# Rings of four blocks, looped edge stages, and own rows added on VectorE in a four-layer graph network

## The chip, the cores and the metric

The kernel runs on one core of a Trainium2 chip. The core has five engines that work side by side, each with its own stream of instructions: PE (TensorE, the matrix engine), DVE (VectorE), ACT (ScalarE), POOL (GpSimd) and SP (SyncE, which here only issues DMAs). Sixteen DMA engines move data between DRAM and the on-chip memories (SBUF, and PSUM for PE's results). Engines wait for each other and for DMAs by semaphores. The metric is the device time of one launch in microseconds (us); lower is better.

## The reference, cut to what matters

There are 100,000 nodes with rows of 128 float32 values, and 50,000 edges sorted by their destination. Four layers follow each other; between layers the features are added to the layer's result and normalised per row. Only the parts that the change touches are told in detail.

- Layer 0: for each node the largest difference to its neighbours, two weight blocks of 128x128, bias, relu.
- Layer 1: two edge attributes are turned into factors by small matrices, `x[src]` is multiplied by them and summed per destination (twice), then some ten 128x128 products with the activation `v * sigmoid(v)`, three of them residual (`h = swish(h @ W_i) + h`), and a norm over all nodes.
- Layer 2: a graph convolution with self-loops: `h = x @ W`, neighbours weighted by `1 / sqrt(deg)` on both sides and summed with the own row, bias, relu.
- Layer 3: `x[src]` times `edge_weight`, summed per destination, times `W`, bias, a row norm with `gamma` and `beta`, relu, added to `x` and normalised.

In layer 2 the kernel keeps rows already multiplied by `1/sqrt(deg)`; the row norm afterwards doesn't see a factor per row. So for a row with edges it computes, up to that factor,

```python
relu((sum_of_source_rows + own_row) @ W2 + sqrt(deg) * b2) + deg * own_row
```

## The kernel before, in words

Rows are worked on in blocks of 512 (four tiles of 128 rows). There are NB = 196 blocks of nodes and EB = 98 blocks of edge rows. A node that is the destination of edges has its true values in the edge row of its last edge, and table `home` says where each node's current row lies. The program is a chain of stages with a barrier between them:

- `setup`: masks, degrees, prepared weights. It stores `sdeg` (the square roots of the degrees) as one float32 row in DRAM. `b2_x3` and `b3_x3` hold a bias as three bfloat16 parts on three partitions, so that three-row bfloat16 products with ones add up to the float32 bias.
- `nodes01`: layer 0 and the products of layer 1 over all node blocks, and each second step one edge block of layer 0. Step `t` works on block `t` and on older blocks at later points of the chain. The last result, `hs[3]`, is stored as `hT` (features by rows).
- `edges1`: layer 1 over the edge blocks, with `q_own`, `q_ea`, `q_cont`, `q_ends` in rings of three blocks and the gathered `q_rows` in four; it also reads `hT` of the nodes again for the statistics of the norm.
- `nodes23`: the norm, then layers 2 and 3 over the nodes.
- `edges2`: layer 2 over the edge blocks.
- `edges3`: layer 3 over the edge blocks, scattering rows into the output.

Each stage is written out by hand per engine as a list of steps; each engine goes through its own instructions in this order and waits for semaphore counts. `after(engine, sem, n)` is a wait for a count that is left out where it isn't positive; `landed(ring, t)` is the count that a slot's DMA semaphore has when block `t`'s transfer is complete. `gather` and `scatter` issue four indirect DMAs of 128 rows of 512 bytes from POOL.

In `nodes01` the engines PE, ACT and DVE run their steps in a hardware loop of four steps a trip (`staggered`: the first 16 steps and the last are written out, the middle is a `Fori`; `Turn` gives the block number as a register in the loop and as a number outside). In `edges1`, `edges2` and `edges3` all steps are written out. SP and POOL are written out everywhere.

The order around `hT` in `nodes01`: DVE's residual add L787 of block n is made in step n+6. It waits for the store of block n-2, as `hs[3]` has two slots. SP's step t issues the load of `x` (block t), in even steps the load of `pen` (L571, after the scan L829 of two DVE steps before), then the stores of `p_o`, `p_oe` and `hT` (L584, block t-9). POOL gathers `p_xs`, writes `home` (L600), raises to the power -0.5 (L610) and gathers `p_xd` in each second step; `nm` (L805) on DVE waits for L610, and L812 to L171 follow it. On PE the three residual products are L640, L660 and L703; L835 on DVE takes the edge block's product of L680.

In `edges2` PE turns the gathered rows and the own rows by transposes (L192), ACT copies the turned own rows from PSUM to `oT` (L1617), and for each of four tiles PE makes three products: one row of `sdeg` with `b2` (L1598), `oT` with `w2` (L1600), `run` with `w2` (L1602), all float32, each as two passes in the trace. DVE makes the scan (L1639), `v` (L1655), statistics (L171) and aggregates (L178). Own rows, `cont` and `sdeg` have rings of four blocks, the gathered rows one of eight.

In `edges3` the order of POOL is: gather of block t, scatter of block t-6. `u_rows` has a ring of eight blocks. The scatter waits for `appliedB`, which ACT reaches in its step e+4.

## Time and profile before

| | |
|---|---|
| median of 3 runs | 6735.22 us (6679.89 to 6737.17) |
| the profiled execution | 6752.29 us, span 6750.5 us |
| busy share of the span | PE 76%, DVE 64%, ACT 51%, POOL 61% |
| mean granted clock of PE | 0.861 of full speed |
| DMA | 956.23 MB, mean 142 GB/s |

Busy times are unions of an engine's instructions. PEld are weight loads, which overlap PE. The granted clock is 1 at 2.4 GHz and 0.5 at 1.2 GHz. After an instruction, square brackets or the part behind the second bar give the idle time of the engine before it and what ended it; "issue" is a wait for nothing that the profile shows, "remote" one ended by something that it can't name. A releaser is inferred from the semaphore that changed last, so a DMA of another stage named there is not the real cause.

### The profile page before, as it was taken

Reading aid. Unit: us, or ns where it says so; the run is one execution under the profiler, and the core shown is the slowest. Engines: PE = TensorE matmul, PEld = TensorE weight load, DVE = VectorE, ACT = ScalarE, POOL = GpSimd, SP = SyncE. Lnnn points to the kernel's source line nnn. Section 1 sums busy time; section 2 is a strip of 40 time slices with the busy share of each in tenths; the row PEclk is TensorE's granted clock in tenths of the full one; section 3 lists DMA queues with packets and bytes.
Section 4 is the critical chain, followed back from the end, with each engine's and each line's share of the span. In section 5 each row is a group of like instructions: output and inputs, shape, how many; then the busy total and the mean of one; then the engine's idle time right before and its main releaser. Section 6 shows DMA issues by size and latency. Waiting matters only on the chain. (4 is left out here: it accounts for less than half of the span.)

```text
span 6750.5 us, 90517 instructions
## 1 busy us (share of the span) xinstructions
PE 5136.1 (76%) x21595; PEld 3187.6 (47%) x21595; DVE 4337.5 (64%) x14214; ACT 3430.8 (51%) x8343; POOL 4146.8 (61%) x4038
## 2 busy tenths in 40 slices
PE   5888888888888886999999878888689973233332
PEld 3455555555555542444444356666477762122221
DVE  4555555555555553777777799999755546555554
ACT  3566666666666652444444367777545543223232
POOL 5555666556666545666666268888755646666666
PEclk9999999999999998999999999999777875555555
DMA  3223333233322233555555489999745532222222
GB/s 87 95 98 103 103 103 99 95 103 103 104 98 97 102 89 77 155 158 159 154 155 157 144 313 360 361 360 359 258 131 141 148 116 70 71 70 71 72 71 58
DMA packets 622084, 956.23 MB, mean 142 GB/s; under 512 B 145416, under 2 KB 238274, under 8 KB 621718
## 3 DMA queue, kind: packets, MB, share of 16 engines
q1 hardware_dynamic: 516358, 801.45, 35.1%
q0 software_dynamic: 100352, 149.23, 9.1%
q8 instruction: 116, 1.90, 0.1%
q10 hardware_dynamic: 5008, 1.60, 0.1%
q14 instruction: 250, 2.05, 0.1%
HBM read 570.69 MB, written 386.68 MB: 142 GB/s over the span
## 5 line engine op out<-in xcount | busy, mean ns | idle before, releaser
L718 ACT ACTIVATE p_s<-p_ps,cols 128x512 f32<-128x512 f32 x588 | 404.0, 687 | 707.0 <-issue 322.7
L787 DVE TENSOR_TENSOR p_r<-p_s,p_r 128x512 f32<-128x512 f32 x588 | 389.2, 687 | 579.2 <-DMA hT<-p_r 369.6
L192 PE MATMUL u_ps_s<-ident,u_weighted 128*128 128x128 f32 x392 | 109.2, 434 | 830.2 <-DVE u_weighted L1770 338.2
L610 POOL TENSOR_TENSOR p_rs<-p_guard,minus_half 128x12 f32<-128x12 f32 (+2 forms) x99 | 246.6, 2491 | 646.2 <-DVE p_guard L860 646.2
L156 POOL DMA_INDIRECT q_rows<-t_rows,home_cols x392 | 391.6, 999 | 368.8 <-PE q_ps L192 266.8
L163 POOL DMA_INDIRECT out<-u_res,scatter_cols x392 | 401.7, 1025 | 297.3 <-ACT u_res L185 183.4
L156 POOL DMA_INDIRECT t_rows<-t_rows,home_cols x392 | 370.1, 944 | 250.6 <-issue 92.9
L156 POOL DMA_INDIRECT u_rows<-t_rows,home_cols x392 | 390.3, 996 | 178.6 <-issue 119.1
L156 POOL DMA_INDIRECT p_xd<-in_x,dst_cols x392 | 429.2, 1095 | 108.7 <-issue 108.7
L600 POOL DMA_INDIRECT home<-edge_row_cols,scatter_cols x392 | 416.1, 1061 | 119.5 <-issue 119.5
L192 PEld LDWEIGHTS u_ps_s<-ident,u_weighted 128*128 128x128 f32 x392 | 70.1, 217 | 859.0 <-DVE u_weighted L1770 351.8
L156 POOL DMA_INDIRECT p_xs<-in_x,src_cols x392 | 373.4, 953 | 149.9 <-issue 119.2
L975 POOL DMA_INDIRECT home_cols<-home,src_cols x392 | 371.8, 948 | 144.7 <-issue 119.2
L660 PE MATMUL p_ps<-p_r,lins 128*128 128x512 f32 x392 | 241.8, 702 | 249.7 <-issue 179.2
L171 DVE BATCH_NORM_STATS2 r_st<-r_v 128x6 f32<-128x128 f32 x1960 | 422.6, 278 | 8.5 <-POOL r_v L1320 1.5
L185 ACT ACTIVATE r_x<-r_v,r_nm,r_rs 128x128 f32<-128x128 f32 x784 | 321.5, 482 | 95.5 <-DVE r_nm L1485 95.5
L1117 DVE TENSOR_TENSOR q_r<-q_s,q_r 128x512 f32<-128x512 f32 x294 | 201.1, 684 | 234.7 <-ACT q_s L1065 163.6
L1334 PE MATMUL r_ps_n<-r_wn,r_h 128*128 128x128 f32 x2352 | 343.1, 289 | 0.0
L185 ACT ACTIVATE p_o<-p_v,p_nm,p_rs 128x128 f32<-128x128 f32 x784 | 321.1, 485 | 16.9 <-DVE p_nm L805 16.9
L1334 PEld LDWEIGHTS r_ps_n<-r_wn,r_h 128*128 128x128 f32 x2352 | 286.9, 192 | 68.4 <-issue 68.4
L185 ACT ACTIVATE u_n<-u_ps_o,u_nmA,u_rsA 128x128 f32<-128x128 f32 x392 | 147.6, 457 | 247.2 <-DVE u_nmA L1806 188.3
L1065 ACT ACTIVATE q_s<-q_ps,cols 128x512 f32<-128x512 f32 x294 | 202.1, 687 | 120.2 <-PE q_ps L997 78.2
(292 smaller groups left out, 15081.5 us busy)
## 6 DMA issues: line engine op xcount, KB each, us to landing
r_h<-hT SPq DMA_DIRECT2D x294, 256.0 KB
r_x<-t_rows SPq DMA_DIRECT2D x294, 256.0 KB
t_rows<-r_y SPq DMA_DIRECT2D x294, 256.0 KB
p_x<-in_x SPq DMA_DIRECT2D x196, 256.0 KB
t_rows<-p_o SPq DMA_DIRECT2D x196, 256.0 KB
hT<-p_r SPq DMA_DIRECT2D x196, 256.0 KB
q_hn<-hT SPq DMA_DIRECT2D x196, 256.0 KB
t_rows<-r_x SPq DMA_DIRECT2D x196, 256.0 KB
```

Of the source, the lines that this page charges most:

```text
L156: nc.gpsimd.indirect_dma_start(out=rows[:, j, :], out_offset=None, in_=table, in_offset=bass.IndirectOffsetOnAxis(ap=idx[:, j:j + 1], axis ...
L163: nc.gpsimd.indirect_dma_start(out=table, out_offset=bass.IndirectOffsetOnAxis(ap=idx[:, j:j + 1], axis=0), in_=rows[:, j, :], in_offset=N ...
L171: i = nc.vector.bn_stats(st[:, j, :], v[:, j, :])
L185: i = nc.scalar.activation(dst[:, j, :], v[:, j, :], ACT.Identity, bias=nm[:, j:j + 1], scale=rs[:, j:j + 1])
L600: nc.gpsimd.indirect_dma_start(out=tab["home"], out_offset=bass.IndirectOffsetOnAxis(ap=s["scat"][:, k:k + 1], axis=0), in_=s["at"][:, k:k ...
L610: nc.gpsimd.tensor_tensor(rs[:, q.of(2), lo:hi], guard[:, q.of(2), lo:hi], s["half"][:, lo:hi], ALU.pow).then_inc(rooted, 1)
L660: nc.tensor.matmul(flat(bank_r), s["lins"][:, 1, :], hs[1][:, n.of(2), :], start=True, stop=True).then_inc(r_done[1], 1)
L718: nc.scalar.activation(act_out[i][:, :], flat(bank_r), ACT.Silu, bias=col(LS0 + i)).then_inc(r_act[i], 1)
L787: nc.vector.tensor_tensor(hs[i + 1][:, n.of(2), :], act_out[i][:, :], hs[i][:, n.of(2), :], ALU.add).then_inc(r_added[i], 1)
L975: nc.gpsimd.indirect_dma_start(out=s["home"][:, k:k + 1], out_offset=None, in_=tab["home"], in_offset=bass.IndirectOffsetOnAxis(ap=s["src" ...
L1065: nc.scalar.activation(act_out[i][:, :], flat(bank_r), ACT.Silu, bias=col(LS0 + i)).then_inc(r_act[i], 1)
L1334: i_mm = nc.tensor.matmul(bank_n[i % 2][:, j, :], h[:, i % 6, tile(j)], wn[:, :], start=False, stop=j == G - 1)
```

## The change

- Rings for `hT`: `hs[3]` and its semaphores `h_saved` have four slots instead of two, in `nodes01` and in `edges1`.
- `edges1`: `own`, `ea`, `cont`, `ends` have four slots instead of three. PE, ACT and DVE run as a loop of four steps a trip (the first 16 steps and the last written out). The order within a step stays.
- `setup`: `sdeg` is split into three bfloat16 parts and stored as nine bfloat16 rows (each part three times); `b2_x9` holds the three parts of the bias three times on nine partitions.
- `edges2`: no `oT`; DVE adds the turned own rows to the scan's result (`both`), and PE multiplies the sum by `w2`; the bias is one bfloat16 product of nine rows. The factors `deg` are copied to `degs` on DVE. `own`, `cont` and `sdeg` have eight slots, `od` four. SP stores block t-8 instead of t-6. The engines run as a loop of eight steps a trip.
- `edges3`: `rows` has four slots instead of eight, `v` four instead of three; some waits stand ahead of the statistics instead of the aggregates; a loop of four steps a trip.
- In the loops DVE waits for its own counts of statistics with a register value, after a wait for 1 (`wait_values`, `first_wait`).

The core of the diff; what is left out rewrites `t % k` and `e` as `t.of(k)` and `e.b` in the same way:

```diff
 class Turn:
+    def twice(self, i):
+
+        return Turn(self.q, 2 * self.slot + i, 2 * self.unroll)
...
 # setup
-            sp.wait_ge(rooted, 1)
-            sp.dma_start(in_rows("sdeg"), sdeg_r[:, :]).then_inc(sdeg_stored, DMA)
+            sp.wait_ge(b2_split, 1)
+            for k in range(3):
+                sp.dma_start(s["b2x9"][3 * k:3 * k + 3, :], s["b2x3"][:, 0, :]).then_inc(b2_copied, DMA)
+            for k in range(9):
+                sp.wait_ge(sdeg_split, 1 + 2 * (k // 3))
+                sp.dma_start(tab["sdeg"][k:k + 1, :].rearrange("o (p t) -> (o p) t", p=P),
+                             sdeg_part[:, k // 3, :]).then_inc(sdeg_stored, DMA)
...
+            dve.wait_ge(rooted, 1)
+            nc.vector.tensor_copy(sdeg_part[:, 0, :], sdeg_r[:, :]).then_inc(sdeg_split, 1)
+            dve.wait_ge(sdeg_split, 1)
+            nc.vector.tensor_tensor(sdeg_left[:, 0, :], sdeg_r[:, :], sdeg_part[:, 0, :], ALU.subtract).then_inc(sdeg_split, 1)
...
 # nodes01 (and the same in edges1)
-        hs = [sb(f"p_r{i}", [P, 2, BLK]) for i in range(4)]
+        hs = [sb(f"p_r{i}", [P, 4 if i == 3 else 2, BLK]) for i in range(4)]
...
-                elif n.past(2):
-                    dve.wait_ge(h_saved[n.of(2)], landed(2, n.back(2)))
-                nc.vector.tensor_tensor(hs[i + 1][:, n.of(2), :], act_out[i][:, :], hs[i][:, n.of(2), :],
+                elif n.past(4):
+                    dve.wait_ge(h_saved[n.of(4)], landed(4, n.back(4)))
+                nc.vector.tensor_tensor(hs[i + 1][:, n.of(4 if i == 2 else 2), :], act_out[i][:, :], hs[i][:, n.of(2), :],
                                         ALU.add).then_inc(r_added[i], 1)
...
 # edges1
+        UNROLL, FIRST, LOOP_TO = 4, 16, EB // 4 * 4
...
-                    after(sp, f_ready, t - 2)
-                    sp.dma_start(ea[:, t % 3, :], a["edge_attr_T"][:, t * BLK:(t + 1) * BLK]).then_inc(ea_in[t % 3], DMA)
+                    after(sp, f_ready, t - 3)
+                    sp.dma_start(ea[:, t % 4, :], a["edge_attr_T"][:, t * BLK:(t + 1) * BLK]).then_inc(ea_in[t % 4], DMA)
...
-            for t in range(STEPS):
+            staggered(pe, FIRST, LOOP_TO, STEPS, UNROLL, step)
...
 # edges2, SP
-                    after(sp, o_turned, t - 3)
-                    after(sp, grown, t - 3)
-                    sp.dma_start(own[:, t % 4], own_v[t]).then_inc(own_in[t % 4], DMA)
+                    after(sp, o_turned, t - 7)
+                    after(sp, grown, t - 7)
+                    sp.dma_start(own[:, t % 8], own_v[t]).then_inc(own_in[t % 8], DMA)
...
-                e = t - 6
+                e = t - 8
...
 # edges2, PE
+                    after(pe, added, t.b - 1)
+                    transpose4(nc, bank_t[t.of(2)], own[:, t.of(8)], s["ident"]).then_inc(o_turned, 1)
...
+                    pe.wait_ge(added, e.b + 1)
                     for j in range(G):
-                        nc.tensor.matmul(bank_o[e % 2][:, j, :], sdeg[:, e % 4, tile(j)], s["b2"][0:1, :],
+                        nc.tensor.matmul(bank_o[e.of(2)][:, j, :], sdeg[:, e.of(8), tile(j)], s["b2x9"][:, :],
                                          start=True, stop=False)
-                        nc.tensor.matmul(bank_o[e % 2][:, j, :], oT[:, e % 2, tile(j)], s["w2"][:, :],
-                                         start=False, stop=False)
-                        i = nc.tensor.matmul(bank_o[e % 2][:, j, :], run[:, e % 2, tile(j)], s["w2"][:, :],
+                        i = nc.tensor.matmul(bank_o[e.of(2)][:, j, :], both[:, e.of(2), tile(j)], s["w2"][:, :],
                                              start=False, stop=True)
...
 # edges2, ACT
-                if t < EB:
-                    act.wait_ge(o_turned, t + 1)
-                    after(act, product, t - 1)
-                    nc.scalar.activation(oT[:, t % 2, :], flat(bank_t[t % 2]), ACT.Copy).then_inc(copied, 1)
...
 # edges2, DVE
+                if t.live(EB):
+                    after(dve, grown, t.b - 1)
+                    nc.vector.tensor_copy(degs[:, t.of(2), :], s["deg"][:, bass.ds(t.b * G, G)]).then_inc(picked, 1)
...
+                if t.live(EB):
+                    dve.wait_ge(scanned, t.b + 1)
+                    dve.wait_ge(o_turned, t.b + 1)
+                    after(dve, product, t.b - 1)
+                    nc.vector.tensor_tensor(both[:, t.of(2), :], run[:, t.of(2), :], flat(bank_t[t.of(2)]),
+                                            ALU.add).then_inc(added, 1)
...
+                    done, = wait_values(e.b + 1)
+                    first_wait(dve, counted)
+                    dve.wait_ge(counted, done)
...
 # edges3
-        RING = 8
+        RING, UNROLL, FIRST, LOOP_TO = 4, 4, 8, EB // 4 * 4
```

## Rows read from the trace of the kernel before

**Rows 1.** Windows: us; busy (count) of PE, PEld, DVE, ACT, POOL; PEclk, DMA, GB/s.
```profile
80.00:2540.00 2460.00, 2113.96 (x8542) 1254.52 (x8542) 1379.20 (x3985) 1504.10 (x2829) 1445.98 (x1258) 0.95 0.30 98
2540.00:2645.00 105.00, 55.08 (x123) 25.02 (x124) 24.22 (x33) 19.28 (x31) 64.70 (x68) 0.73 0.30 61
2645.00:3870.00 1225.00, 1164.34 (x3217) 542.78 (x3215) 942.24 (x1325) 548.73 (x854) 685.35 (x704) 1.00 0.52 151
3870.00:4854.00 984.00, 806.44 (x5196) 602.85 (x5196) 938.35 (x5047) 661.18 (x2652) 749.64 (x785) 0.97 0.97 344
4854.00:4911.00 57.00, 19.88 (x67) 15.81 (x68) 2.50 (x2) 3.52 (x10) 37.82 (x40) 0.50 0.28 81
4911.00:5530.00 619.00, 591.38 (x3070) 471.02 (x3069) 351.93 (x1272) 330.16 (x970) 332.29 (x352) 0.81 0.49 139
5530.00:6750.00 1220.00, 358.24 (x1274) 254.19 (x1274) 666.89 (x2450) 353.40 (x980) 791.91 (x784) 0.50 0.24 70
```

**Rows 2.** The scans, by tile: count, shortest/median/longest ns, first and last start.
```profile
L829 DVE TENSOR_TENSOR_SCAN p_run<-p_pen,p_run,p_ps x97: 1266/1273/1279, 91.4 to 2480.8; 128x512 f32<-128x512 bf16 x97
...
L1170 DVE TENSOR_TENSOR_SCAN q_run<-q_cont,q_run,q_m x97: 1273/1276/1277, 2583.2 to 3844.0; 128x512 f32<-128x512 bf16 x97
...
L1639 DVE TENSOR_TENSOR_SCAN t_run<-t_cont,t_run,t_ps_s x97: 1278/1280/1282, 4867.2 to 5514.7; 128x512 f32<-128x512 bf16 x97
...
L1796 DVE TENSOR_TENSOR_SCAN u_run<-u_cont,u_run,u_ps_s x97: 1249/1279/1281, 5544.6 to 6705.0; 128x512 f32<-128x512 bf16 x97
```

**Rows 3.** Groups by line, 100 to 2400 us: busy, mean ns | idle before, releasers.
```profile
L600 POOL DMA_INDIRECT home<-edge_row_cols,scatter_cols x371 | 394.2, 1062 | 113.1 <-issue 113.1
...
L787 DVE TENSOR_TENSOR p_r<-p_s,p_r 128x512 f32<-128x512 f32 x553 | 365.6, 687 | 546.6 <-DMA hT<-p_r 358.9 <-issue 167.1 <-ACT p_s L718 20.1
...
L610 POOL TENSOR_TENSOR p_rs<-p_guard,minus_half 128x12 f32<-128x12 f32 x92 | 230.7, 2507 | 594.6 <-DVE p_guard L860 594.6
```

**Rows 4.** Timeline of VectorE (DVE): start, us, instruction, idle before and releaser.
```profile
1108.56 1.29 DVE L787 TENSOR_TENSOR p_r<-p_s,p_r 128x512 f32<-128x512 f32 x2 [5.59 <-DMA hT<-p_r]
...
1115.22 0.69 DVE L835 TENSOR_TENSOR p_ve<-p_ps,b_row 128x512 f32<-128x512 f32 x1 [2.54 <-remote]
```

**Rows 5.** SP's queue: its waits in total, and one issue on the timeline.
```profile
SPq L571 <- DVE p_run L829: 1722.6, 85, 24.2
...
1103.66 0.46 SPq L584 DMA_DIRECT2D hT<-p_r  x1
```

**Rows 6.** Timeline of PE in the first stage.
```profile
1109.91 1.12 PE L660 MATMUL p_ps<-p_r,lins 128*128 128x512 f32 x2 [2.83 <-issue]
...
1125.46 1.13 PE L703 MATMUL p_ps<-p_r,lins 128*128 128x512 f32 x2 [0.72 <-DVE p_r L787]
...
1134.32 1.13 PE L660 MATMUL p_ps<-p_r,lins 128*128 128x512 f32 x2 [2.97 <-issue]
```

**Rows 7.** Timeline at the start of `edges2`: PE, then GpSimd (POOL).
```profile
4903.27 0.37 PE L1598 MATMUL t_ps_o<-b_row,t_sdeg 1*128 1x128 f32 x1 [2.43 <-issue]
...
4911.33 0.94 POOL L156 DMA_INDIRECT t_rows<-t_rows,home_cols  x1 [6.93 <-DMA t_rows<-r_x]
```

**Rows 8.** Timeline in `edges3`: VectorE, then GpSimd.
```profile
5984.20 0.38 DVE L178 BATCH_NORM_AGGREGATE u_mvA<-u_stA 128x2 f32<-128x6 f32 x4 [4.75 <-DMA t_rows<-r_x]
...
6003.49 1.01 POOL L163 DMA_INDIRECT out<-u_res,scatter_cols  x1 [6.53 <-ACT u_res L185]
```

**Rows 9.** Timeline of PE in `edges2`; then, by line, the bfloat16 bias of `edges3`.
```profile
5301.71 0.79 PE L1598 MATMUL t_ps_o<-b_row,t_sdeg 1*128 1x128 f32 x2
...
5305.32 1.06 PE L192 MATMUL t_ps_s<-ident,t_rows 128*128 128x128 f32 x4
5306.17 1.06 PE L192 MATMUL t_ps_t<-ident,t_own 128*128 128x128 f32 x4
...
L1730 PE MATMUL u_ps_o<-b_x,ones 3*128 3x512 bf16 x94 | 56.6, 603 | 0.0
```

**Rows 10.** Timeline of VectorE in the setup: the cast of a 128x392 row block.
```profile
5.01 1.56 DVE L427 CAST cont_bf<-cont_f 128x392 bf16<-128x392 f32 x1
```

More of the change, by code:

```diff
@@ L1032, in _ @@
[L1032 to L1038 removed]
+                    pe.wait_ge(own_in[t.of(4)], landed(4, t))
+                    transpose4(nc, bank_t, own[:, t.of(4)], s["ident"]).then_inc(turned, 1)
@@ new lines, in step @@
+                if n.live(EB):
+                    dve.wait_ge(r_added[2], n.b + 1)
+                    dve.wait_ge(ends_in[n.of(4)], landed(4, n))
+                    after(dve, e_counted, n.b)
+                    nc.vector.tensor_tensor(last[:, :], hs[3][:, n.of(4), :], ends[:, n.of(4), :], ALU.mult).then_inc(masked, 1)
+                for i in range(2):
+                    n = t.back(DENSE_LAG).twice(i)
+                    if n.live(NB):
+                        dve.wait_ge(hn_in[n.of(4)], landed(4, n))
+                        dve.wait_ge(nmask_in[n.of(4)], landed(4, n))
+                        after(dve, n_counted, n.b - 1)
+                        nc.vector.tensor_tensor(hm[:, n.of(2), :], hn[:, n.of(4), :], nmask[:, n.of(4), :],
@@ L1724, in _, with step @@
         def _(pe):
-            for t in range(EB + 2):
-                e = t - 2
-                if live(e, EB):
-                    pe.wait_ge(scanned, e + 1)
-                    after(pe, appliedA, e - 1)
-                    nc.tensor.matmul(flat(bank_o[e % 2]), s["ones3"][:, :], s["b3x3"][:, :, :].rearrange("o j f -> o (j f)"),
+            def step(t):
+                e = t.back(2)
+                if e.live(EB):
+                    pe.wait_ge(scanned, e.b + 1)
+                    after(pe, appliedA, e.b - 1)
+                    nc.tensor.matmul(flat(bank_o[e.of(2)]), s["ones3"][:, :], s["b3x3"][:, :, :].rearrange("o j f -> o (j f)"),
```

685 lines of the change are left out of this document (349 added, 336 removed).

## The prediction

> **What bounds the kernel now.** I first read the windows by stage [rows 1]. Their seven stretches are layers 0 and 1 over the nodes (2,460 us), the beginning and the rest of the layer 1 edge stage (105 and 1,225 us), layers 2 and 3 over the nodes (984 us), the beginning and the rest of the layer 2 edge stage (57 and 619 us), and the layer 3 edge stage (1,220 us). No engine bounds all of them, so I read each stage by itself. The scans, one a block, give its rhythm [rows 2]: (2480.8 - 91.4)/96 = 24.9 us for a pair of node blocks in the first stage, (3844.0 - 2583.2)/96 = 13.1 us a block in `edges1`, (5514.7 - 4867.2)/96 = 6.7 us in `edges2`, (6705.0 - 5544.6)/96 = 12.1 us in `edges3`.
>
> In the first stage PE is busy 86% of the time. Grouping its instructions by line shows why it isn't more: VectorE's residual add L787 sat idle for 546.6 us in the 2,300 us shown, 358.9 of them put down to the store of `hT` [rows 3]. The timeline shows one instance: VectorE stands still for 5.59 us before an L787 at 1108.56 [rows 4], waiting for the store that SP issued at 1103.66 [rows 5]. That store can't be issued sooner, since SP's queue stands behind the load of `pen`, which waits for the scan (1,722.6 us in total, 85 times [rows 5]). PE then has its own gap of 2.83 us before L660 (called issue; it starts 0.06 us after the second L787 of that row ends), and every second step a smaller one of 0.72 us before L703 [rows 6]. In between PE runs back to back.
>
> The second thing to see is what happens when GpSimd issues indirect DMAs without a pause. At the start of `edges2` PE falls to one matmul every 2.8 us, with no wait in the code between them, and is itself again only when GpSimd has been still for some us: its next gather comes after 6.93 us [rows 7]. In `edges3` VectorE waits 4.75 us between its own statistics and its own aggregate (put down to a DMA that had long ended); GpSimd later pauses 6.53 us [rows 8], and steps of about 7 us follow. I call this the crawl. The rows show when it comes, not why.
>
> **The ring of `hT`, layers 0 and 1.** `hs[3]` and `h_saved` go from two blocks to four. L787 in step T then needs the store of block T-10. SP issues that after the scan of step T-3 at the latest (odd block) or T-4 (even), so with the 4.9 us that the store took to free VectorE it has over 20 us of slack. The 5.59 us stall goes. What is late next: PE, which has work without a gap. The pair takes 24.4 us in the instance shown (the same L660 comes at 1109.91 and 1134.32 [rows 6]); without 2.83 and 0.72 us, and without the tenth of a us that each restart costs, it is 20.7. But VectorE's L835 had 2.54 us of idle time put down to no engine of this core [rows 4], which fits a beginning crawl near the end of GpSimd's run, and GpSimd's L610 (2.5 us [rows 3]) stands before `nm`. I keep one gap of 0.7 us, and 0.2 us for stretches at the lower clock: 21.6. GpSimd doesn't bound it: 1445.98 us of work [rows 1] are 14.8 a pair, and its twelve indirect DMAs have 0.3 us ahead of each (L600, 113.1/371 [rows 3]), 18.4 in all. So 98 x (24.9 - 21.6) = 323 us less. Bounds: 20.7 gives 412 less; if only PE's 2.83 us of gap went half away, 139 less.
>
> **`edges1` as loops, rings of four.** PE is busy 95% of the steady stretch at full clock [rows 1]. Rings for `own`, `ea`, `cont`, `ends` and `hT` free nothing that it waits for. The order of PE, ScalarE and VectorE stays. A loop replaces immediate wait values by registers and adds a return every four steps; the first stage is already looped so, and of its trips of two pairs none can lose over 1 us at the return, as the mean pair of 24.9 is 0.5 above the one of [rows 6], which has no gap beyond the two named. Cost 0, bounds -25 (the 5% not busy, half of it) to +50 us (0.5 us a step if registers cost on PE). The crawl at its beginning (105 us for some four blocks) comes from GpSimd's own unchanged order, and stays.
>
> **`edges2`.** On PE a block loses sixteen fp32 passes (four bias products and four with `oT`, two each). At the lower clock six products took 3.61 us (from L1598 at 5301.71 to the transposes at 5305.32 [rows 9]), 0.60 each, so 8 x 0.6 = 4.8 us go. Four bfloat16 products of nine rows come back. The nearest row is L1730: 603 ns for one bfloat16 product of 512 columns [rows 9], so 0.15 to 0.6 us each; I take 0.2, nearest by columns, 0.8 in all. ScalarE loses the 0.6 us copy. VectorE gains a 128x512 add with PSUM (0.69, as L787 [rows 3]) and a copy of four columns (0.15): its block is then about 4.9 us, from 351.93/96 = 3.7 busy [rows 1] plus 0.85 and the waits on itself. PE at the lower clock: transposes 2 x 0.85 [rows 9], products 4 x 0.6 + 0.8, some 4.9. GpSimd issues four gathers: 332.29/352 = 0.94 plus the 0.3 of every issue, 5.0 us. All three meet at 4.9 to 5.1, and then GpSimd has no pause, which is the condition of the crawl. In `edges3`, where that holds, eight indirect DMAs take 12.1 us, 1.5 each; four of these are 6.0 us. So 6.0 a block where the 619 us gave about 6.4 for 96: 40 us less. Bounds: 5.1 a block, 130 less; 6.9, 45 more. Rings of eight change nothing here, as PE didn't wait for loads. SP's store moves two steps later, behind three loads that wait for blocks seven back, all done by then; ScalarE needs its slot four steps on.
>
> **`edges3`.** GpSimd needs 791.91/784 + 0.3 = 1.31 us for each indirect DMA [rows 1], 10.5 a block; the rest of 12.1 is crawl, in which VectorE falls back after steps of 7. The ring of eight for gathered rows is cut to four. That adds no wait: in GpSimd's queue the gather stands behind a scatter of a block six back, which already needs VectorE at step t-3, and the ring asks for step t-4. The loops don't touch GpSimd. Its run length and the crawl stay: 0. Bounds: -155 us (98 x 1.6, no crawl at all), +30 (0.3 us a step for registers and the slices of `ew`).
>
> **Setup.** Five VectorE instructions of 128x392, at most 1.56 us each as the cast L427 [rows 10], and twelve small DMAs on SP beside them; the end of the stage is VectorE's tail. +3 us, as the other instructions there are shorter (0 to +8). The layer 2 and 3 node stage isn't touched.
>
> **The sum** is made on the profiled execution: 6,752 us, span 6,750.5. -323 + 0 - 40 + 0 + 3 = -360, so 6,392. It stood 17 us above the median of the runs shown; I carry that over: 6,375 us. Runs lay 0.8% apart, so about 1% is what a measurement here can tell from no change.
>
> **Rivals.** (a) The loops end the crawl: it would be the engines' instruction supply, which straight code of `edges1` to `edges3` strains. For it: the looped first stage shows none of the long stalls. Against: that stage's GpSimd pauses for 9 us a pair (594.6/92 = 6.5 of wait and L610's 2.5 [rows 3]), the matmuls of [rows 7] did run, slowly, and one to one with GpSimd's run. Then `edges3` goes to 10.5 a block (-155) and `edges2` to 5.1 (-90 beyond mine): 6,130. Chance 0.15.
> (b) Another wait takes the store's place in the first stage, most likely `nm` behind L610 and the delayed product: half the gain, 6,375 + 160 = 6,535. Chance 0.17.
> (c) The loop's return costs a stall each time. The nearest row is PE's gap of 2.83 us [rows 6], if that were one: 20 + 11 + 22 returns make 53 x 2.8 = 150 us, 6,525. Chance 0.06. The Trainium skill, "Runtime: NRT & Kernel Launch", Instruction fetch mechanics, has such a rule: code is prefetched in sequence only, and a taken branch out of the two pages held makes the engine wait for the target, a reason to prefer unrolled code. The looped first stage doesn't show it.
> (d) Slower than before: the faster first stage itself starts the crawl. GpSimd would be at work 18.4 of 21.6 us, 85%, near `edges3`'s 10.5 of 12.1. There eight DMAs cost 12.1 - 7 = 5 us beyond a free step; twelve would cost 7.5, and a pair would take 29.1 instead of 24.9: +412 us, 7,110. It decides from 3.3 us of crawl a pair on. Against it: L610 and the wait after the run leave 5 to 6 us without a DMA issued in every pair, while `edges3`'s runs between pauses last some 30 us. Chance 0.07.
> (e) My forecast, 6,375: 0.55.
>
> **Range and chances.** 6,130 to 6,580: it takes in (a), (b), (c) and the bounds of `edges2`, and leaves out (d) and the far ends. Faster by over 1% in (a), (b), (c), (e) but for combinations of small gains: 0.89; within 1%: 0.04; slower: 0.07.
>
> **What would show it.** The wait of L787 for `hT` gone and PE over 95% busy in the first stage, pairs at 21 to 22 us; `edges1` at 13 us a block; in `edges2` PE half idle and GpSimd the busiest, at about 6 us a block, VectorE's idle time put down to odd releasers; `edges3` still with steps of 7 and of 20 us. I am wrong if pairs stay above 23 us, if the crawl has gone from `edges3`, or if gaps recur every four or eight steps.

## The result, and the profile after

The changed kernel took 6642.42 us (median, 6630.32 to 6655.74) where the kernel before took 6726.91 (6679.89 to 6737.17): ratio 0.989, 95% interval 0.986 to 0.991. That is 84 us less and not the 360 forecast. The profiled execution has a span of 6639.2 us, 111.3 less. The scans give the rhythm again, one row a stage (by tile: count, shortest/median/longest ns, first and last start), as [rows 2]:

```profile
L853 DVE TENSOR_TENSOR_SCAN p_run<-p_pen,p_run,p_ps x97: 1262/1273/1279, 97.3 to 2414.0; 128x512 f32<-128x512 bf16 x97
...
L1201 DVE TENSOR_TENSOR_SCAN q_run<-q_cont,q_run,q_m x97: 1274/1276/1277, 2518.0 to 3769.5; 128x512 f32<-128x512 bf16 x97
...
L1676 DVE TENSOR_TENSOR_SCAN t_run<-t_cont,t_run,t_ps_s x97: 1269/1280/1283, 4794.6 to 5390.3; 128x512 f32<-128x512 bf16 x97
...
L1853 DVE TENSOR_TENSOR_SCAN u_run<-u_cont,u_run,u_ps_s x97: 1267/1280/1281, 5419.0 to 6595.7; 128x512 f32<-128x512 bf16 x97
```

Over these 97 scans the first stage takes 2,316.7 us where it took 2,389.4, so 73 less: 24.13 us a pair instead of 24.9, where I had forecast 21.6. `edges1` gives 9 us less, `edges2` 52 less (6.2 us a block, forecast 6.0), `edges3` 16 more (12.3, forecast 12.1). So all but one of the terms are near their forecasts, and the first stage isn't. The windows (columns as in [rows 1]) show that stage, then the rest of `edges2`:

```profile
69.00:2424.00 2355.00, 2061.43 (x8534) 1203.98 (x8535) 1380.14 (x3972) 1485.97 (x2813) 1442.96 (x1252) 0.97 0.31 102
...
4836.00:5391.00 555.00, 474.51 (x1890) 345.63 (x1890) 407.64 (x1426) 281.35 (x849) 332.58 (x352) 0.60 0.53 151
```

PE is busy 88% of the first stage, not over 95%. Grouped by line over the same stretch as [rows 3], the idle time has moved (first the changed kernel, then the edge product's add in the kernel before):

```profile
L811 DVE TENSOR_TENSOR p_r<-p_s,p_r 128x512 f32<-128x512 f32 x571 | 384.2, 686 | 181.5 <-issue 101.9 <-ACT p_s L742 74.1
...
L664 PE MATMUL p_ps<-p_r,lins 128*128 128x512 f32 x382 | 223.6, 669 | 234.3 <-DVE p_r L865 231.0 <-ACT p_s L742 3.3
...
L859 DVE TENSOR_TENSOR p_ve<-p_ps,b_row 128x512 f32<-128x512 f32 x95 | 65.7, 692 | 463.8 <-remote 463.8
```

```profile
L835 DVE TENSOR_TENSOR p_ve<-p_ps,b_row 128x512 f32<-128x512 f32 x92 | 63.6, 691 | 231.9 <-remote 116.8 <-PE p_ps L680 114.8
```

The residual add (L811, L787 before) no longer waits for the store; its idle time falls from 546.6 to 181.5 us. But the add of the edge product (L859, L835 before) stands idle for 463.8 us, 4.9 us each time, put down to nothing on this core. Before, it was 231.9 us, half of it put down to the product itself. PE's L664 loses 2.4 us each time behind it. The timeline of one pair, GpSimd, then VectorE, then PE:

```profile
1202.95 2.30 POOL L634 TENSOR_TENSOR p_rs<-p_guard,minus_half 128x12 f32<-128x12 f32 x1 [5.93 <-DVE p_guard L884]
1205.44 1.03 POOL L160 DMA_INDIRECT p_xd<-in_x,dst_cols  x1 [0.19 <-issue]
...
1220.71 0.98 POOL L624 DMA_INDIRECT home<-edge_row_cols,scatter_cols  x1 [0.30 <-issue]
...
1227.17 2.70 POOL L634 TENSOR_TENSOR p_rs<-p_guard,minus_half 128x12 f32<-128x12 f32 x1 [5.47 <-DVE p_guard L884]
...
1223.01 0.69 DVE L859 TENSOR_TENSOR p_ve<-p_ps,b_row 128x512 f32<-128x512 f32 x1 [4.75 <-remote]
...
1226.91 0.17 DVE L884 TENSOR_SCALAR p_guard<-p_mv 128x12 f32<-128x12 f32 x1
...
1201.23 1.87 PE L669 MATMUL p_ps<-p_xx,R 128*128 128x512 f32 x2
...
1217.91 0.39 PE L704 MATMUL p_ps<-w_neg,p_run 128*128 128x128 f32 x2
...
1224.41 1.37 PE L664 MATMUL p_ps<-p_r,lins 128*128 128x512 f32 x2 [2.24 <-DVE p_r L865]
```

PE's last edge product ends at 1217.91 + 0.39 = 1218.30. VectorE, which waits only for it, starts at 1223.01: the signal came 4.7 us late, and 1.3 us after GpSimd's last indirect DMA (1220.71 + 0.98). So the pair is a ring of its own: 2.5 us from the power (L634) to the first DMA, 16.2 of twelve DMAs, 1.3 until the signals come through, 4.2 on VectorE up to the guard and L634 again: 24.2 us. After each gap PE's products also run slower for a while (L669 at 1201.23 takes 1.87 us, later ones 1.02). The kernel before had the same ring; its timeline of GpSimd, then VectorE, then PE, in the pair of [rows 4], is

```profile
1095.22 2.29 POOL L610 TENSOR_TENSOR p_rs<-p_guard,minus_half 128x12 f32<-128x12 f32 x1 [5.91 <-DVE p_guard L860]
1097.71 1.03 POOL L156 DMA_INDIRECT p_xd<-in_x,dst_cols  x1 [0.19 <-issue]
...
1112.42 1.11 POOL L600 DMA_INDIRECT home<-edge_row_cols,scatter_cols  x1 [0.30 <-issue]
1119.38 2.70 POOL L610 TENSOR_TENSOR p_rs<-p_guard,minus_half 128x12 f32<-128x12 f32 x1 [5.85 <-DVE p_guard L860]
...
1119.12 0.17 DVE L860 TENSOR_SCALAR p_guard<-p_mv 128x12 f32<-128x12 f32 x1
...
1112.87 0.39 PE L680 MATMUL p_ps<-w_neg,p_run 128*128 128x128 f32 x2
```

24.16 us from power to power, in the same legs: 2.5 us to the first DMA, 15.8 of twelve DMAs (to 1113.53), 1.7 until VectorE's L835 starts (1115.22, [rows 4]), 4.2 to the next power. The store's stall lay inside the time in which GpSimd was issuing anyway. The ring was a floor and not yet the bound of every pair: the mean was 24.9, and from one power to the next no pair took under 24.1 us but the last two of the stage.

### The profile page after: what moved, and what is told of

Read it like the earlier page. It is cut to its first block and busy times, and to the rows that moved or that the text cites. A ratio compares the mean times of both kernels' runs of the same rounds, so it can differ in the third digit from the quotient of the medians.

```text
span 6639.2 us, 91378 instructions
## 1 busy us (share of the span) xinstructions
PE 4979.3 (75%) x20419; PEld 3008.4 (45%) x20419; DVE 4417.4 (67%) x14415; ACT 3384.8 (51%) x8245; POOL 4154.8 (63%) x4038
## 3 DMA queue, kind: packets, MB, share of 16 engines
q8 instruction: 62, 1.02, 0.1%
## 5 line engine op out<-in xcount | busy, mean ns | idle before, releaser
L634 POOL TENSOR_TENSOR p_rs<-p_guard,minus_half 128x12 f32<-128x12 f32 (+2 forms) x99 | 246.3, 2488 | 575.0 <-DVE p_guard L884 575.0
L811 DVE TENSOR_TENSOR p_r<-p_s,p_r 128x512 f32<-128x512 f32 x588 | 395.9, 687 | 199.7 <-issue 101.9
L160 POOL DMA_INDIRECT p_xs<-in_x,src_cols x392 | 394.3, 1006 | 152.8 <-issue 119.3
L624 POOL DMA_INDIRECT home<-edge_row_cols,scatter_cols x392 | 391.6, 999 | 119.5 <-issue 119.5
L664 PE MATMUL p_ps<-p_r,lins 128*128 128x512 f32 x392 | 229.1, 668 | 235.2 <-DVE p_r L865 231.0
L859 DVE TENSOR_TENSOR p_ve<-p_ps,b_row 128x512 f32<-128x512 f32 x98 | 67.8, 692 | 466.8 <-remote 465.8
L1635 PE MATMUL t_ps_o<-w,t_both 128*128 128x128 f32 x784 | 284.5, 462 | 0.0
```

The costliest lines, as they stand in the source:

```text
L160: nc.gpsimd.indirect_dma_start(out=rows[:, j, :], out_offset=None, in_=table, in_offset=bass.IndirectOffsetOnAxis(ap=idx[:, j:j + 1], axis ...
L624: nc.gpsimd.indirect_dma_start(out=tab["home"], out_offset=bass.IndirectOffsetOnAxis(ap=s["scat"][:, k:k + 1], axis=0), in_=s["at"][:, k:k ...
L634: nc.gpsimd.tensor_tensor(rs[:, q.of(2), lo:hi], guard[:, q.of(2), lo:hi], s["half"][:, lo:hi], ALU.pow).then_inc(rooted, 1)
L664: nc.tensor.matmul(flat(bank_r), s["lins"][:, 0, :], hs[0][:, n.of(2), :], start=True, stop=True).then_inc(r_done[0], 1)
L811: nc.vector.tensor_tensor(hs[i + 1][:, n.of(4 if i == 2 else 2), :], act_out[i][:, :], hs[i][:, n.of(2), :], ALU.add).then_inc(r_added[i], 1)
L1635: i = nc.tensor.matmul(bank_o[e.of(2)][:, j, :], both[:, e.of(2), tile(j)], s["w2"][:, :], start=False, stop=True)
```

## The experiments

Lines of code are diffs against the changed kernel, unless said otherwise. The experiments ran in seven groups, each with the kernel before beside it. Five groups ran on chips on which the kernel before takes 6,342 to 6,354 us (four chips), two on chips where it takes 6,721 and 6,760, near the 6,727 of the result. I call the first kind calm and say at each experiment which it was. On the chips with the crawl every kernel ran in one execution only. The theories named are: A, the length of GpSimd's run of indirect DMAs holds back the other engines' signals; B, the scatters of 4-byte rows do; C, it depends on the chip and not on the kernel alone.

**1. The ring undone (`n01_ring2`, calm).** `h_saved` goes back to two as well.

```diff
-        hs = [sb(f"p_r{i}", [P, 4 if i == 3 else 2, BLK]) for i in range(4)]
+        hs = [sb(f"p_r{i}", [P, 2, BLK]) for i in range(4)]
```

> The changed kernel with the ring of hT in the first stage set back to two blocks, all else as changed. If the ring's own worth in that stage is what the two traces show, the wait of VectorE's third residual add for the store comes back, a pair goes from 24.2 to 24.9 us, and the kernel takes some 70 us more, 6,710. If the ring is worth nothing and the 70 us came from elsewhere (the order of semaphores, another clock), it takes 6,640.

6266.15 us, ratio 0.985 (0.981 to 0.989), 24.2 us a pair. It is neither of the two times expected, as this chip is a calm one. The changed kernel itself took 5907 us on this chip (experiment 5), so the ring of four is worth 359 us there.

**2. The scatters moved (`n01_mid`, calm).** The loop over `nc.gpsimd.indirect_dma_start(out=tab["home"], ...)` moves:

```diff
                     gather(nc, xs[:, e % 2], a["x"], s["src"][:, e * G:(e + 1) * G], xs_in[e % 2])
-                    for j in range(G):
-                        nc.gpsimd.indirect_dma_start(out=tab["home"], ...)
...
                     gather(nc, xd[:, e % 2], a["x"], s["dst"][:, e * G:(e + 1) * G], xd_in[e % 2])
+                    for j in range(G):
+                        nc.gpsimd.indirect_dma_start(out=tab["home"], ...)
```

> The four scatters of home stand between the gathers of xd and those of the next xs, so that GpSimd's run of twelve indirect DMAs is as long as before, and ends with gathers. Theory A, the length of the run holds back the other engines' semaphore updates near its end: VectorE's add of the edge product still stands idle for 4.7 us until the run ends, the pair stays at 24.2 us, 6,640. Theory B, it is the scatters of 4-byte rows that hold them back: the stall leaves the end of the run and shows 6 to 11 us after L634, before other instructions; at the end VectorE waits under 1 us.

5901.01 us, 0.928 (0.924 to 0.932); 20.3 us a pair.

**3. A pause (`n01_pause`, calm).**

```diff
                     gather(nc, xs[:, e % 2], a["x"], ...)
+                    after(pool, paused, e)
+                    nc.gpsimd.iota(pause[:, :], pattern=[[1, BLK]], base=0, channel_multiplier=1).then_inc(paused, 1)
                     for j in range(G):   # home
```

> One iota of 128x512 (some 1.6 us, as 128x784 took 2.4) on GpSimd between the gathers of xs and the scatters of home, which cuts the run into eight and four DMAs. Theory A (the length of the run): the 4.7 us stall goes, PE is the bound, a pair takes 21 to 22 us, the kernel 6,640 - 97 x 2.5 = 6,400. Theory B (the scatters): the stall stays and ends 1.6 us later, a pair takes 25.8, 6,790. If GpSimd's own cycle is the bound whatever else happens, the same 25.8.

5907.24 us, 0.928 (0.925 to 0.932), 20.3 us a pair; one iota took 0.57 us, not 1.6.

**4. All scatters ahead (`n01_front`, calm).**

```diff
+            for e in range(EB):
+                for j in range(G):
+                    nc.gpsimd.indirect_dma_start(out=tab["home"], ...)
             for t in range(QB + 1):
```

> All 392 scatters of home are issued by GpSimd ahead of the first gather: some 392 x 1.3 = 510 us in which nearly nothing else runs, and after that runs of eight gathers. Theories A and B both have the stall before the add of the edge product gone and a pair at 21 to 22 us: 6,640 + 510 - 260 = 6,890. If instead something else than GpSimd's DMAs makes the 4.7 us (the product itself, the loop), a pair stays at 24.2 and it takes 7,150.

6400.92 us, in one execution: the scatters cost 500, the pair 20.3. On their face, 2 speaks for theory B, 3 for theory A and 4 for both, and that was the warning: in none of the four traces was there any crawl, not even in `edges3` (10.2 us a block), and the kernel before beside them took 6,353. They had to be set against the changed kernel itself on such a chip.

**5. The two kernels themselves on a calm chip, and 2 again (`after_again`, `before_again`, `n01_mid_again`).**

> The changed kernel once more, beside the kernel before, since the four kernels tried so far and the kernel before beside them (6,353 us against 6,727) showed no crawl in any stage. Theory C, the crawl belongs to the chip or the hour and not to the kernel: without it, the changed kernel has pairs of 20.3 us in the first stage, no 4.7 us stall, 5.0 us a block in layer 2's edge stage and 10.1 in layer 3's, and takes about 5,900 us, 0.93 of the kernel before; where the crawl is there, 6,640, 0.99. Theory A or B (GpSimd's order makes the stall always): pairs of 24.2 us also where the rest shows no crawl, about 6,270.

> The kernel before, unchanged, for a trace of it on the same chip as the run of the changed kernel. Theory C: without the crawl the first stage has 24.4 us a pair by the store's stall alone, layer 1's edge stage 12.8 us a block with no long stall at its beginning, layer 2's 5.4 to 6, layer 3's 10.1, in all 6,350; with the crawl the times by stage of the profile before.

> The kernel with the scatters of home between the gathers of xd and of xs once more. Without the crawl on this chip: the same as the changed kernel within 0.5%, as PE bounds both. With it: theory A (length of GpSimd's run) 6,640 and the stall of 4.7 us at the end of the run still there; theory B (the scatters) the stall elsewhere or gone, 6,640 to 6,300.

The changed kernel took 5906.89 us, ratio **0.930 (0.928 to 0.932)**; the kernel before in one profiled execution 6331.48 us (span 6329.8); the one with the moved scatters 5902.73, 0.929 (0.927 to 0.932). Scans of the kernel before, then of the changed one:

```profile
L829 DVE TENSOR_TENSOR_SCAN p_run<-p_pen,p_run,p_ps x97: 1261/1275/1279, 84.4 to 2397.4; 128x512 f32<-128x512 bf16 x97
...
L1639 DVE TENSOR_TENSOR_SCAN t_run<-t_cont,t_run,t_ps_s x97: 1279/1280/1282, 4732.8 to 5224.4; 128x512 f32<-128x512 bf16 x97
...
L1796 DVE TENSOR_TENSOR_SCAN u_run<-u_cont,u_run,u_ps_s x97: 1279/1280/1281, 5254.3 to 6284.2; 128x512 f32<-128x512 bf16 x97
```

```profile
L853 DVE TENSOR_TENSOR_SCAN p_run<-p_pen,p_run,p_ps x97: 1264/1274/1279, 87.8 to 2039.2; 128x512 f32<-128x512 bf16 x97
...
L1676 DVE TENSOR_TENSOR_SCAN t_run<-t_cont,t_run,t_ps_s x97: 1279/1280/1281, 4373.3 to 4854.9; 128x512 f32<-128x512 bf16 x97
...
L1853 DVE TENSOR_TENSOR_SCAN u_run<-u_cont,u_run,u_ps_s x97: 1279/1280/1281, 4884.7 to 5868.2; 128x512 f32<-128x512 bf16 x97
```

Pairs go from 24.1 to 20.3 us (-362 over the 97 scans), `edges2` from 5.12 to 5.02 a block (-10), `edges3` from 10.7 to 10.2 (-46), and `edges1` stays at 12.8 and 12.7. GpSimd's timeline of the changed kernel there:

```profile
1239.35 0.98 POOL L624 DMA_INDIRECT home<-edge_row_cols,scatter_cols  x1 [0.30 <-issue]
1242.29 2.70 POOL L634 TENSOR_TENSOR p_rs<-p_guard,minus_half 128x12 f32<-128x12 f32 x1 [1.95 <-DVE p_guard L884]
```

It waits 1.95 us instead of 5.5 to 5.9 between its run of twelve and the power, and L859 stood idle for 11.9 us in 94 pairs instead of 463.8. PE is then busy 99% of the first stage at full clock, as the forecast had it (columns as in [rows 1]):

```profile
69.00:2049.00 1980.00, 1961.74 (x8534) 1171.99 (x8535) 1391.33 (x3973) 1492.77 (x2814) 1428.04 (x1252) 1.00 0.37 121
```

The same program, the same run of DMAs: what holds signals back isn't there. Theory C holds: the crawl isn't a property of the kernel alone. Windows of the rest of `edges2`, before, then changed, each from its own trace:

```profile
4750.00:5225.00 475.00, 474.81 (x2982) 380.15 (x2981) 337.51 (x1211) 316.29 (x932) 348.08 (x369) 1.00 0.64 180
```

```profile
4380.00:4856.00 476.00, 443.94 (x1905) 322.76 (x1903) 409.40 (x1428) 283.79 (x856) 353.76 (x374) 0.65 0.63 179
```

Before, PE is the bound at full clock (1.00). The change takes a third of its instructions away, its clock falls to 0.65, and GpSimd's gathers, (353.76/374 + 0.3) x 4 = 5.0 us a block, bound it at the same pace.

**6. Single parts on a calm chip (`ring_alone`, `straight`, `straight_r8`).** The first is the kernel before with only `nodes01` changed:

```diff
-        hs = [sb(f"p_r{i}", [P, 2, BLK]) for i in range(4)]
+        hs = [sb(f"p_r{i}", [P, 4 if i == 3 else 2, BLK]) for i in range(4)]
```

and `h_saved` likewise. The other two are the changed kernel with `for t in range(last): step(Turn(t // unroll, t % unroll, unroll))` for `staggered` in `edges1` to `edges3`; the last has `RING = 8` in `edges3` too.

> The kernel before with nothing but the ring of four for hT in the first stage. Where the crawl is absent (kernel before at 6,350): if that ring carries the gain, pairs of 20.3 us instead of 24.0, 6,353 - 97 x 3.7 = 5,990, ratio 0.943, and the rest of the change is worth some 80 us. If loops or the other rings do part of it, over 6,100. Where the crawl is there (kernel before at 6,730): pairs of 24.2, some 6,660.

> The changed kernel with the loops of the three edge stages written out as straight code again, rings as changed. My forecast had loops at nothing: 5,907 us without the crawl, within 20, and edges3 at 10.2 us a block. Rival: the loops carry the 47 us that layer 3's edge stage gained (10.65 to 10.17 a block), through the supply of instructions: 5,955, edges3 at 10.6. With the crawl: 6,640, the crawl as in the changed kernel.

> As the kernel with the three loops undone, and layer 3's edge stage also has its ring of eight for the gathered rows back. If the ring of four set another phase between VectorE and GpSimd there and so shortened the indirect DMAs (1.08 to 1.00 us of GpSimd each), 10.6 us a block comes back: 5,955. If neither ring nor loop matters, 5,907. With the crawl: 6,640, and steps of 7 and 20 us.

The ring alone gives 5976.22 us, 0.942 (0.939 to 0.946), 20.4 us a pair: 369 us less than the kernel before beside it, where the whole change gave 446 on the chip of experiment 5. Without the loops the rest takes 5938.69, 0.936 (0.933 to 0.940); with the ring of eight besides, 5936.11, 0.936 (0.932 to 0.939). The changed kernel itself didn't run in this group; on two other calm chips it took 5907 and 5908. So the ring of gathered rows is worth nothing and the loops some 30 us, all in `edges3` (10.6 us a block in straight code, 10.2 looped). That stage is bound by GpSimd's eight DMAs, which took 1.07 to 1.08 us each in the kernel before, 1.05 in both kernels of straight code and 1.00 in the looped one. The kernel before, then the looped one:

```profile
L156 POOL DMA_INDIRECT u_rows<-t_rows,home_cols x181 | 195.7, 1081 | 55.2 <-issue 55.2
L163 POOL DMA_INDIRECT out<-u_res,scatter_cols x182 | 194.9, 1071 | 55.5 <-issue 55.5
```

```profile
L167 POOL DMA_INDIRECT out<-u_res,scatter_cols x192 | 191.9, 1000 | 58.5 <-issue 58.5
L160 POOL DMA_INDIRECT u_rows<-t_rows,home_cols x192 | 191.6, 998 | 58.5 <-issue 58.5
```

Why they are shorter in the looped kernel stays open. The ring of gathered rows isn't it, as the last kernel shows; another phase between VectorE and GpSimd is a guess.

**7. Cuts with one iota (`probe1`, `probe2`, calm).** The pause of experiment 3 at the places that the expectations name, as here in `edges3` (`probe1`):

```diff
                     gather(nc, rows[:, t % RING], tab["t3"], s["home"][:, t * G:(t + 1) * G], rows_in[t % RING])
+                after(pool, paused, t)
+                nc.gpsimd.iota(pause[:, :], pattern=[[1, BLK]], base=0, channel_multiplier=1).then_inc(paused, 1)
                 e = t - AHEAD
```

> The changed kernel with GpSimd's runs cut in four places, to be read stage by stage: first stage with the scatters of home in the middle of the run (as n01_mid); layer 1's edge stage with an iota of 128x512 (1.6 us) between its four home gathers and its four row gathers in blocks 2 to 11; layer 2's edge stage with one after every eight gathers; layer 3's with one between gathers and scatters of every block. Where the crawl is there (kernel before at 6,730) and theory A holds (the length of the run): no stalls of 20 to 40 us at the beginning of layers 1 and 2, 5.8 us a block in edges2 and 12.1 in edges3, both regular, 6,530 in all. Theory B (something else starts it): the stalls stay and the iotas come on top, over 6,800. Where the crawl isn't there (kernel before at 6,350): only the iotas' price, 0.8 x 98 + 1.6 x 98 + at most 16: 5,907 + 250 = 6,155.

> The same question with other cuts: first stage with the iota between the gathers of xs and the scatters (as n01_pause), layer 1's edge stage as changed (control), layer 2's with an iota after every four gathers, layer 3's with one every second block. With the crawl, theory A: pairs of 21 to 22 us in the first stage, the stall at the beginning of edges1 as in the changed kernel (36 us), none in edges2 at 6.6 us a block, edges3 11.3 to 12.2: 6,480. Theory B: 24.2 or more a pair, over 6,750. Without the crawl: 5,907 + 1.6 x 98 + 0.8 x 98 = 6,140.

5981.15 and 5972.93 us. They met no crawl, so they only show the price: `edges3` takes 10.8 us a block with an iota a block (`probe1`), `edges2` 5.4 (`probe2`).

**8. Added traffic, and 2 again (`load`, `n01_mid_third`, chip with the crawl).** The copies:

```diff
+            for k in range(8):
+                nc.scalar.dma_start(tab["junk"][k], a["x"][k * 24 * BLK:(k + 1) * 24 * BLK, :]...).then_inc(copied_away, DMA)
```

> The changed kernel with extra copies from DRAM to DRAM, issued on ScalarE's queue at the beginning of three stages: eight of 6.3 MB each in the first stage (rows of x), eight in layer 2's and eight in layer 3's edge stage (blocks of hT). Nobody waits for them before the stage's end. Theory D, the crawl is contention with other traffic on the DMA engines or HBM: while the copies run, PE shows gaps that no wait explains (a matmul every 2.8 us), semaphore updates come late, and pairs of 24 us or more, edges2 over 6, edges3 over 12 us a block. Theory E, traffic alone doesn't do it: transfers take longer, so that single waits on loads may grow, but signals between engines stay under 0.2 us and the first stage, whose loads are issued a step ahead, stays near 20.3 to 22 us a pair.

> The kernel with the scatters in the middle of GpSimd's run, in case this chip has the crawl. Without it (kernel before at 6,350): 5,903, as twice before. With it (6,730): theory A 24.2 us a pair with 4.7 us of stall at the end of the run, theory B no stall there.

The kernel before took 6760.05 us here, the one with the copies 7071.57, the one with the moved scatters 6692.47. Since the crawl was there without the copies, D and E aren't told apart: inconclusive. The pairs took 24.75 us with the copies, `edges2` 6.6 and `edges3` 12.7 us a block. The moved scatters are telling. Timeline of GpSimd, VectorE, PE:

```profile
1211.55 1.02 POOL L160 DMA_INDIRECT p_xd<-in_x,dst_cols  x1 [0.19 <-issue]
...
1226.91 0.95 POOL L160 DMA_INDIRECT p_xs<-in_x,src_cols  x1 [0.30 <-issue]
...
1229.30 0.69 DVE L859 TENSOR_TENSOR p_ve<-p_ps,b_row 128x512 f32<-128x512 f32 x1 [4.93 <-remote]
...
1224.03 0.39 PE L704 MATMUL p_ps<-w_neg,p_run 128*128 128x128 f32 x2
```

The run now ends with gathers, and the signal of L704 (ends 1224.42) still comes 4.9 us late, 1.4 us after the run's end; 24.4 us a pair. Theory B has fallen.

**9. The length of the run (`n01_front_again`, `probe3`, chip with the crawl).** The second has three iotas into three slices at each place (`for c in range(3): nc.gpsimd.iota(pause[:, c, :], ...)`).

> The kernel with all scatters of home ahead of the loop, so that GpSimd issues runs of eight gathers in the first stage. With the crawl (kernel before at 6,760), theory A, the delay begins some ten indirect DMAs after the run's start: no stall before L859, 20.3 to 21 us a pair in the steady stretch, while edges1 to edges3 show the crawl as before (13.4, 6.2, 12.2 us a block). Rival F, any run of indirect DMAs holds back the signals that fall near its end: 24 us a pair still. Without the crawl (6,350): 20.2 a pair and 6,401 in all, as before.

> The changed kernel with pauses of three iotas (0.57 us each, 1.7 in all) on GpSimd: in the first stage between the gathers of xs and the scatters, in layer 1's edge stage in blocks 2 to 11 between home gathers and row gathers, in layer 2's after every eight gathers, in layer 3's between gathers and scatters. With the crawl, theory A and the pause long enough to end a run: 21 to 22 us a pair, no stalls of 20 to 40 us at the beginning of edges1 and edges2, 5.9 a block in edges2, 12.2 in edges3, all regular, some 6,400. If 1.7 us of pause doesn't end a run: as the changed kernel or slower, 6,640 to 6,800. Without the crawl (6,350): 20.3, 12.8, 5.9 and 12.0, 6,180.

The kernel before took 6720.60 us. With all scatters ahead, runs are of eight DMAs and pairs take (2574.7 - 625.8)/96 = 20.3 us. The second fence has VectorE, then PE, near the end of a run of eight (its last DMA ends at 1609.20):

```profile
L854 DVE TENSOR_TENSOR_SCAN p_run<-p_pen,p_run,p_ps x97: 1262/1275/1279, 625.8 to 2574.7; 128x512 f32<-128x512 bf16 x97
```

```profile
1608.08 0.69 DVE L837 TENSOR_TENSOR p_v<-p_ps,b_row 128x512 f32<-128x512 f32 x1 [1.28 <-issue]
...
1606.89 1.05 PE L679 MATMUL p_ps<-w,p_xT 128*128 128x128 f32 x8
```

The edge product itself ends 1.8 us after such a run (1611.04) and so says nothing of rival F. But PE's L679 ends at 1607.94 within the run, and VectorE's L837, which waits for it, starts 0.14 us later: this signal near the end of a run of eight isn't held back, and F has fallen for the first stage. At the same time the crawl is there in the later stages (`edges3` at 12.1 a block). 6792.41 us in all, 500 of them for the scatters ahead. With the pauses, 6232.41 us:

```profile
L857 DVE TENSOR_TENSOR_SCAN p_run<-p_pen,p_run,p_ps x97: 1264/1274/1278, 91.9 to 2042.0; 128x512 f32<-128x512 bf16 x97
...
L1210 DVE TENSOR_TENSOR_SCAN q_run<-q_cont,q_run,q_m x97: 1274/1276/1277, 2131.0 to 3381.5; 128x512 f32<-128x512 bf16 x97
...
L1690 DVE TENSOR_TENSOR_SCAN t_run<-t_cont,t_run,t_ps_s x97: 1279/1280/1281, 4407.7 to 5006.7; 128x512 f32<-128x512 bf16 x97
...
L1872 DVE TENSOR_TENSOR_SCAN u_run<-u_cont,u_run,u_ps_s x97: 1279/1280/1281, 5036.8 to 6179.8; 128x512 f32<-128x512 bf16 x97
```

and its timeline of GpSimd, then VectorE, at the cut:

```profile
1217.61 0.94 POOL L160 DMA_INDIRECT p_xs<-in_x,src_cols  x1 [0.30 <-issue]
1218.57 1.61 POOL L625 IOTA p_pause<- 128x512 int32 x3
1220.36 1.08 POOL L628 DMA_INDIRECT home<-edge_row_cols,scatter_cols  x1 [0.18 <-issue]
...
1220.45 0.68 DVE L863 TENSOR_TENSOR p_ve<-p_ps,b_row 128x512 f32<-128x512 f32 x1
```

1.6 us of other work for GpSimd per pair, and the add of the edge product (L863) doesn't wait: 20.3 us a pair, as on a calm chip. `edges3` takes 11.9 a block, which is the calm 10.2 plus the pause, and no more steps of 7 and 20. `edges2` (6.2) gained nothing over the changed kernel as a whole: its long first step shrank from 41 to at most 12 us, but ten steps near the beginning take 7 to 12 us each. Signals are late there in spite of runs of eight and pauses of 1.6 us: PE's product of one block ends at 4447.34, and VectorE takes it at 4449.83.

`edges1` still has a step of 34 us (36 in the changed kernel), but where the cuts end. Its pauses stand in blocks 2 to 11, the last iota starts at 2206.9, and up to there no step takes over 14.7 us. Then GpSimd issues 40 indirect DMAs without a pause (2207.64 to 2260.08), and the long step, from 2220.4 to 2254.3, lies in this run. So there too it comes with the uncut run. Pauses in more blocks were not tried where the crawl is. Theory A has held for the first stage, fits `edges1`, and explains `edges2` only in part.

**10. The cut kernel beside the changed one (`cut_runs`, `after_third`, calm).** The pauses of three iotas in every pair of the first stage, in blocks 2 to 11 of `edges1`, and after every second of the first twelve blocks of `edges2`:

```diff
                 gather(nc, rows[:, t % RING], tab["t2"], s["home"][:, t * G:(t + 1) * G], rows_in[t % RING])
+                if t < 12 and t % 2 == 1:
+                    after(pool, paused, 3 * (t // 2))
+                    for c in range(3):
+                        nc.gpsimd.iota(pause[:, c, :], pattern=[[1, BLK]], base=0, channel_multiplier=1).then_inc(paused, 1)
```

> The changed kernel with the pauses of 1.7 us on GpSimd in the first stage (every run), in layer 1's edge stage in blocks 2 to 11, and in layer 2's after every eight gathers of the first twelve blocks; layer 3's as changed. With the crawl (kernel before at 6,740): first stage 97 x 3.9 = 378 us less than the changed kernel, the beginnings of edges1 and edges2 18 and 25 us less: 6,642 - 421 = 6,220, ratio 0.925. Without it (6,350): the changed kernel's time + 0 to 20, 5,907 to 5,927, ratio 0.93. If the pauses only move the stall: over 6,500 with the crawl.

> The changed kernel beside it. With the crawl 6,642, ratio 0.9886, pairs of 24.2; without it 5,907, ratio 0.930, pairs of 20.3.

5918.36 us, 0.931 (0.929 to 0.934), and 5908.24, 0.930 (0.927 to 0.932): the cuts cost 10 us where there is no crawl, which is no difference that these runs can tell. Where the crawl is, this kernel has not run; `probe3`, with the same first stage, took 6232 there, 7.3% less than the kernel before beside it, in one execution each.

## Why the prediction was wrong

- **What failed is the sentence "What is late next: PE"** and with it the size of the first term: 24.9 to 21.6 us a pair, 323 us, with bounds of 139 and 412. Under the crawl it was 24.9 to 24.1, 73 us. I took the stall of 5.59 us out of a pair as if nothing else closed a ring around it. GpSimd's power, run of twelve, late signal and VectorE's way to the guard already made 24.16 us in the trace before. The evidence was in my own rows: the 2.54 us before L835, put down to nothing on the core [rows 4]. The product that it waited for ended at 1113.26, so 2.0 us of the 2.54 were a signal held back until 1.7 us after the run's end; before the change the product ended 15.5 us into GpSimd's run, late itself by the store's stall, and after it 12.9, and the same signal came 4.7 us late. I called it "a beginning crawl" and gave it 0.7 us. I also checked GpSimd only as a sum of work (18.4 us), not as a ring with others in it.
- **Rival (b)** had the right kind of mechanism and named the delayed product, at half the gain (6,535). It was four fifths of the gain. Its chance of 0.17 was too low.
- **The mechanism of the ring was right.** L787's wait for the store went, as forecast, and where nothing holds signals back the pair takes 20.3 us and the ring alone saves 369 us of the kernel's time (experiments 5 and 6). There the first term came out at 362 us against 323: neither the gap of 0.7 us nor the 0.2 us for a lower clock, which the forecast had kept, was there (granted clock 0.95 before, 1.00 after).
- **`edges2`**: forecast 40 us less, measured 52, on the calm chip 10. The pace was 6.2 us a block, not 6.0; the gain is still larger because the forecast started from 6.4 (the window of 619 us), where the scans give 6.7 [rows 2]. That GpSimd's gathers bound the block held on the calm chip. PE's clock, which the forecast took as the lower one, fell with its work (0.81 to 0.60, on the calm chip 1.00 to 0.65).
- **`edges3`**: forecast 0 (bounds -155 to +30), measured +16 under the crawl and -46 without it, of which the loops give some 30 (experiment 6); in my sum loops stood at nothing. **`edges1`** and **setup**: 9 less and 2.5 more (the first scan at 69.7 instead of 67.2), within their bounds.
- **Rival (a)**, loops end the crawl, has fallen: `edges3` kept its steps of 7 and 20 us with them. So has **(c)**: no gap recurs at the loop's return (`edges1` keeps steps of 12.7 us), and looped code was some 30 us faster than straight code. The rule of the Trainium skill that I cited there, "Runtime: NRT & Kernel Launch", Instruction fetch mechanics, speaks of a branch whose target lies outside the two pages held; no run here shows such a stall. **(d)**, slower than before, didn't happen: the add of the edge product stood idle twice as long as before (463.8 us against 231.9), yet the pair became no longer.

## What to carry to other kernels

Before a stall is priced as its own length, find the other rings of waits that go through the other engines and sum the longest: if it is nearly as long as the step, as the 24.2 us of a mean pair of 24.9 here, most of the stall is cover and not cost. An idle time of one or two us "put down to nothing" before an instruction whose producer has ended can be such a ring's trace. And a gain may depend on the chip: set the two kernels side by side on several before its size is believed, since here the same change is worth 1.1% on one chip and 7.0% on two others.

## What the runs showed of the hardware

- **On some of the chips met, a run of twelve indirect DMAs on GpSimd in the first stage holds back other engines' signals until it ends.** There a PE signal 11.1 us into the run still came through (the transposes at 1215.91 of the changed kernel's trace, seen by ScalarE at 1216.70), one 12.9 us into it didn't, and was seen 1.3 us after the run's end. In the first stage's runs of eight, or of eight and four with 1.6 us of iotas between, the add of the edge product didn't wait. PE itself went on; only who waited for it stood. On four other chips the same runs, and on the one traced for experiment 5 also some hundred gathers in a row at the beginning of `edges2`, held back nothing, and the kernel before took 6,350 instead of 6,740 us. Whether it goes with the chip, its neighbours' work or the hour stays open, as each chip but one was met once and the added traffic met a chip that had it anyway.
- In longer runs the signals don't wait for the end. At the beginning of `edges2` the changed kernel's GpSimd issues 40 gathers without a pause, from 4779.26 to 4829.04. VectorE and PE there:

```profile
4799.06 0.69 DVE L1688 TENSOR_TENSOR t_both<-t_run,t_ps_t 128x512 f32<-128x512 f32 x1 [3.21 <-remote]
4825.62 0.69 DVE L1700 SCALAR_TENSOR_TENSOR t_v<-t_ps_o,t_od 128x512 f32<-128x512 f32 x1 [25.87 <-issue]
...
4794.32 1.06 PE L196 MATMUL t_ps_t<-ident,t_own 128*128 128x128 f32 x4
4810.90 0.37 PE L196 MATMUL t_ps_t<-ident,t_own 128*128 128x128 f32 x1 [2.43 <-issue]
```

  The turned own rows are ready at 4795.38, 16 us into the run, and VectorE takes them 3.7 us later; the product of the first block ends at 4799.15 and is taken 26 us later, 3.4 us before the run's end. Here the crawl is also more than late signals: PE makes one matmul in 2.8 us without a wait in the code. In `edges1` it doesn't: PE stands still instead, once for 6.4 us with nothing to show for it. None of this was isolated.
- PE's granted clock in `edges2`, on the calm chip, was 1.00 with PE busy all the time and 0.65 once a third of its instructions were gone, and the pace of the stage was nearly the same (5.12 and 5.02 us a block).
